# Bias products as weighted sums on GpSimd, weight maxima in slices, and the output weights' product in other banks

## The reference

```python
h = jnp.maximum(_layernorm(x, axis=-1), 0.0)
q = h @ Wq.T + bq
k = key @ Wk.T + bk
v = value @ Wv.T + bv
scores = jnp.einsum('nd,md->nm', q, k) / scale          # scale = 4096 ** 0.5
adj_scores = scores * adj_matrix
adj_scores = jnp.where(jnp.abs(adj_scores) < 1e-05, -1000000000.0, adj_scores)
prob = jax.nn.softmax(adj_scores, axis=-1)
out = x + jnp.einsum('nm,md->nd', prob, v) @ Wm.T + bm
```

## Time and profile before

| | us |
|---|---|
| median of 3 runs | 1592.18 |
| the profiled execution | 1591.07 |
| its span in the profile | 1589.3 |
| PE busy | 1567.6 (99%) |
| DVE busy | 993.6 (63%) |
| ACT busy | 609.3 (38%) |
| POOL busy | 101.8 (6%) |

### The profile page before, as it was taken

The page is one execution under the profiler, slowest core; times in us unless marked ns, Lnnn a source line. Parts: engine busy times, 40 slices in busy tenths (PEclk is TensorE's granted clock), DMA queues, the critical chain, the costliest instruction groups (busy, mean ns, idle before and its releaser), DMA issues.

```text
span 1589.3 us, 23599 instructions
## 1 busy us (share of the span) xinstructions
PE 1567.6 (99%) x7246; PEld 720.3 (45%) x7246; DVE 993.6 (63%) x2325; ACT 609.3 (38%) x964; POOL 101.8 (6%) x178
## 2 busy tenths in 40 slices
PE   8899999999999999999999999999999999999998
PEld 5543444444444444444444444444444444444443
DVE  4779766656666656656665656666566666666652
ACT  4667333333333333333333333333333333333332
POOL 0132000000000000000000000000000000000000
PEclk9999999999999999999999999999999999999999
DMA  9724555655555455555545555545555554555545
GB/s 348 254 53 107 121 130 117 130 126 125 119 125 124 116 136 119 124 125 127 117 116 137 119 123 122 130 120 119 135 123 119 121 129 119 126 129 124 116 95 106
DMA packets 430287, 205.46 MB, mean 129 GB/s; under 512 B 375088, under 2 KB 375344, under 8 KB 430128
## 3 DMA queue, kind: packets, MB, share of 16 engines
q1 hardware_dynamic: 429680, 204.80, 54.2%
q10 hardware_dynamic: 576, 0.27, 0.1%
HBM read 105.13 MB, written 8.39 MB: 71 GB/s over the span
## 4 chain that ended last, share of the span: by engine, by line
PE 93%; DVE 2%; DMA 2%; issue 1%; ACT 1%; SPq 1%; POOL 0%; DVEq 0%; ACTq 0%; POOLq 0%
PE R L559 13%; PE R L560 13%; PE R L561 13%; PE S L559 13%; PE S L560 13%; PE S L561 13%; PE M L559 3%; PE M L561 3%; PE M L560 3%; DMA pT<-ph 1%; PE R L638 1%; PE R L671 0%; DMA xq<-in_x_dram 0%; DVE small L1142 0%; PE W L709 0%
## 5 line engine op out<-in xcount | busy, mean ns | idle before, releaser
L941 ACT ACTIVATE drop<-Zbuf 128x512 f32<-128x512 f32 x256 | 161.2, 630 | 808.4 <-DVE cmx L1234 808.3
L1225 DVE SCALAR_TENSOR_TENSOR Zbuf<-S,rs,adjb 128x512 f32<-128x512 f32 x256 | 192.0, 750 | 346.4 <-PE S L561 342.6
L559 PE MATMUL R<-Vbuf,pT 128*128 128x512 f16 x1008 | 383.0, 380 | 6.9 <-issue 5.5
L560 PE MATMUL S<-Kbuf,qT 128*128 128x512 f16 x1024 | 388.9, 380 | 0.0
L559 PE MATMUL S<-Kbuf,qT 128*128 128x512 f16 x1024 | 388.8, 380 | 0.0
L561 PE MATMUL S<-Kbuf,qT 128*128 128x512 f16 x1024 | 388.7, 380 | 0.0
L560 PE MATMUL R<-Vbuf,pT 128*128 128x512 f16 x1008 | 382.9, 380 | 0.0
L561 PE MATMUL R<-Vbuf,pT 128*128 128x512 f16 x1008 | 382.8, 380 | 0.0
L1234 DVE CUSTOM_DVE_ANT_0 Zbuf<-drop,Zbuf 128x512 f32<-128x512 f32 x256 | 175.8, 687 | 0.0
L1285 DVE TENSOR_SCALAR drop<-drop,rs 128x512 f32<-128x512 f32 x256 | 142.1, 555 | 33.4 <-ACT drop L941 33.1
L947 ACT ACTIVATE Zbuf<-Zbuf,smx 128x1024 f32<-128x1024 f32 x128 | 157.4, 1230 | 4.5 <-DVE smx L1248 1.6
(11 more groups left out here) (189 smaller groups left out, 1194.2 us busy)
## 6 DMA issues: line engine op xcount, KB each, us to landing
adjb<-in_adj_dram SPq DMA_DIRECT2D x256, 256.0 KB, 2.8
xq<-in_x_dram SPq DMA_DIRECT2D x32, 256.0 KB, 2.8
Kbuf<-in_L_gnn_key_dram SPq DMA_DIRECT2D x8, 1024.0 KB, 14.3
xr<-in_x_dram SPq DMA_DIRECT2D x32, 256.0 KB, 2.8
...
```

Of the source, the lines that this page charges most:

```text
L559: nc.tensor.matmul(ps, lhs[0], rhs[0], start=start, stop=False)
L560: nc.tensor.matmul(ps, lhs[0], rhs[1], start=False, stop=False)
L941: nc.scalar.activation(drop[:, :], Zbuf[:, s.p, s.c * CW:(s.c + 1) * CW], ACT.Abs).then_inc(abs_ready, 1)
L1225: nc.vector.scalar_tensor_tensor(out=z, in0=S[s.j % 2][:, :], scalar=rs[:, r, 3, s.c // 2:s.c // 2 + 1], in1=adjb[:, s.j % ADJ_SLOTS, :], ...
```

## The change

The bias columns are no longer widened. The three bias vectors are loaded as rows on one partition, TensorE turns them into columns with 12 one-row matmuls between 8 and 4 warm-up matmuls (20 before), and VectorE copies the columns out. GpSimd multiplies the four row groups of a weight matrix by its four bias columns and adds them up (`weighted_sum`: four multiplications and three additions of 128 x 512), and one fp32 matmul against ones (`sum_over_partitions`) gives the finished row; this holds for `qbias`, `wrow` and bv Wm^T. The product bq.bk is one product by ones as well. bm is loaded later, by SyncE.

VectorE takes the weight maxima in eight reductions of 512 columns as the weights arrive, instead of two of 2048 after the last, and it does so ahead of the first block's layer norm. The maxima of A go through bank W[1], and those of VB through O[0]. The key scales K2 and K3 are flattened, reduced and spread in other steps: the spread stands one step later than the flattening. Wm is transposed in step 6, bv Wm^T finished in step 10, B formed in steps 7 to 10 in the banks M1, W[0], O[1] and M0, and split in steps 10 and 11; the VB maximum is in steps 8 and 9. The first two adjacency tiles are loaded ahead of key chunk 5, the second query block ahead of Wm, and values in smaller portions a step later in the queue.

```diff
-        wrow, once = W[1], M0[:, 0:1]
...
+        wrow, once = W[1], W[1][:, 0:1]
...
-            FILLS += ["Wm^T"] * ND * (g == 6) + [g] * ND
-        FILLS += ["bias"] + ["B"] * ND
+            FILLS += [g] * ND
+        FILLS += ["Wm^T"] * ND + ["B"] * ND
...
+        B_BANKS = [M1, W[0], O[1], M0]
         def bank_of(n):
-            if FILLS[n] == "bias":
-                return M1
-            return ROUND.get(n // ND, RING)[(n - (FILLS[n] == "B")) % ND]
+            if FILLS[n] == "B":
+                return B_BANKS[n - FILLS.index("B")]
+            return ROUND.get(n // ND, RING)[n % ND]
...
-        WM_STEP, BIAS_STEP, B_STEPS, B_OUT = 4, 5, {6: 0, 7: 1, 8: 2, 9: 3}, 10
-        VB_LARGEST, VB_SCALES = 7, 8
-        V_LOADS = [(1, 2), (3, 4), (5, 6), (7, 8, 9)]
+        WM_STEP, SUM_STEP, BIAS_STEP, B_STEPS, B_OUT = 6, 7, 10, {7: 0, 8: 1, 9: 2, 10: 3}, (10, 11)
+        VB_LARGEST, VB_SCALES = 8, 9
+        V_LOADS = [(1,), (2,), (3,), (4, 5), (6, 7, 8, 9)]
...
+        def top_bank(what):
+            return {"A": W[1], "VB": O[0]}.get(what, M1)
...
             for g in range(NC):
+                if g == ADJ_TURN:
+                    for t in range(ADJ_SLOTS):
+                        load_adj(0, t, t)
                 sp.dma_start(k_stage(g), kv[g, :, :, :]).then_inc(k_in[g], 16)
-            for t in range(ADJ_SLOTS):
-                load_adj(0, t, t)
+            sp.wait_ge(dot_done, 1)
+            sp.dma_start(xq[:, :], x[P:2 * P, :]).then_inc(x_in, 16)
...
+            def weighted_sum(total, term, weights, k, bias, done):
+                nonlocal steps
+                if k == 0:
+                    nc.gpsimd.tensor_scalar(total, weights, bias[:, 0:1], None, ALU.mult).then_inc(sum_steps, 1)
+                    steps += 1
+                else:
+                    wait(pool, sum_steps, steps)
+                    nc.gpsimd.tensor_scalar(term, weights, bias[:, k:k + 1], None, ALU.mult).then_inc(sum_steps, 1)
+                    steps += 1
+                    pool.wait_ge(sum_steps, steps)
+                    last = nc.gpsimd.tensor_tensor(total, total, term, ALU.add)
+                    if k == ND - 1:
+                        last.then_inc(done, 1)
+                    else:
+                        last.then_inc(sum_steps, 1)
+                        steps += 1
...
+            pool.wait_ge(bcol, 1)
+            for k in range(ND):
+                pool.wait_ge(w_in[k], 32)
+                weighted_sum(sum_q, term, Wk_sb[:, k, :], k, bqc, q_sum)
+                if k == ND - 2:
+                    rstd_of(1)
...
+            pool.wait_ge(q_sum, 1)
+            for k in range(ND):
+                if k == 1:
+                    root_of("K0")
+                weighted_sum(sum_w, term, Wq_sb[:, k, :], k, bkc, w_sum)
             root_of("K1")
...
+                if isinstance(s.t, int) and s.t == SUM_STEP:
+                    pool.wait_ge(wm_seen, 1)
+                    pool.wait_ge(start_act, ND)
+                    pool.wait_ge(w_sum, 1)
+                    for k in range(ND):
+                        weighted_sum(sum_o, term_o, WmT[:, k, :], k, bvc, o_sum)
...
                     filled(last)
+            def sum_over_partitions(ps, part):
...
             def out_bias():
-                ps = bank_of(fill)
+                pe.wait_ge(o_sum, 1)
+                pe.wait_ge(v_small, 1)
                 pe.wait_ge(q_small, Q_SMALL + 1)
-                pe.wait_ge(start_act, ND)
-                for k in range(ND):
-                    last = nc.tensor.matmul(ps[:, :], bvrep[:, k, :], WmT[:, k, :], start=(k == 0), stop=(k == ND - 1))
-                filled(last)
+                sum_over_partitions(O[0][:, :], sum_o).then_inc(bias_mm, 1)
...
             pe.wait_ge(ident_ready, 2)
-            for n in range(20):
+            for n in range(8):
+                nc.tensor.matmul(S[1][:, 0:P], ident[:, :], ident[:, :], start=True, stop=True)
+            pe.wait_ge(b_in, 48)
+            for n, b in enumerate(bias_rows):
+                for k in range(ND):
+                    last = nc.tensor.matmul(M0[:, n * ND + k:n * ND + k + 1], b.rearrange("a (p k) -> a k p", k=ND)[:, k, :], one,
+                                            start=True, stop=True)
+            last.then_inc(bcol_mm, 1)
+            for n in range(4):
                 nc.tensor.matmul(S[1][:, 0:P], ident[:, :], ident[:, :], start=True, stop=True)
             for k in range(ND - 1):
                 pe.wait_ge(w_in[k], 32)
                 round_a(k, range(ND))
             pe.wait_ge(w_in[ND - 1], 32)
+            flat_max("A", wmax[:, 0:2], 2)
             round_a(ND - 1, range(0, 1))
-            pe.wait_ge(ident_ready, 2)
...
+            flat_max("K0", kst[:, 6, 0:1], 1)
+            spread_max("A")
+            pe.wait_ge(bcol, 1)
             transpose_x(1)
-            round_a(ND - 1, range(1, 3))
-            spread_max("A")
-            round_a(ND - 1, range(3, 4))
-            flat_max("K0", kst[:, 6, 0:1], 1)
+            round_a(ND - 1, range(1, ND))
+            pe.wait_ge(q_sum, 1)
+            sum_over_partitions(S[1][:, :], sum_q).then_inc(aside_mm, 1)
+            pe.wait_ge(a_small, 1)
+            pe.wait_ge(bdot_ready, 2)
+            sum_over_partitions(once, bdot[:, ND:ND + 1]).then_inc(aside_mm, 1)
+            spread_max("K0")
             transpose_key(0)
-            spread_max("K0")
-            pe.wait_ge(reps_ready, 1)
-            for k in range(ND):
...
+                    if s.t == 3:
+                        spread_max("K3")
...
-                    if s.t == 0:
-                        spread_max("K2")
                     if s.t == 2:
-                        spread_max("K3")
+                        flat_max("K3", kst[:, 6, 3:4], 1)
...
-            dve.wait_ge(b_in, 48)
-            dve.wait_ge(ident_ready, 2)
-            for k in range(ND):
-                nc.vector.tensor_scalar(bqrep[:, k, :], ident[:, :], 0.0, bqc[:, k:k + 1], ALU.mult, ALU.add)
-                nc.vector.tensor_scalar(bkrep[:, k, :], ident[:, :], 0.0, bkc[:, k:k + 1], ALU.mult, ALU.add)
-                last = nc.vector.tensor_scalar(bvrep[:, k, :], ident[:, :], 0.0, bvc[:, k:k + 1], ALU.mult, ALU.add)
-            last.then_inc(reps_ready, 1)
...
+            nc.vector.tensor_reduce(bdot[:, ND:ND + 1], bdot[:, 0:ND], X, ALU.add).then_inc(bdot_ready, 1)
             for k in range(ND):
                 dve.wait_ge(w_in[k], 32)
-            largest(0, (Wq_sb, Wk_sb)).then_inc(part_max, 1)
-            widest_product("A", 2)
-            scale_of(ast, a_small, "A", 400, 2.0 ** -40, 2 * TOP / D, D / (2 * TOP) / HS)
+                for n, w in enumerate((Wq_sb, Wk_sb)):
+                    nc.vector.tensor_reduce(wpart[:, n * ND + k:n * ND + k + 1], w[:, k, :], X, ALU.max,
+                                            apply_absolute_value=True).then_inc(w_part, 1)
+            dve.wait_ge(w_part, 2 * ND)
+            nc.vector.tensor_reduce(wmax[:, 0:2], wpart.rearrange("p (n k) -> p n k", n=2), X, ALU.max).then_inc(part_max, 1)
...
+            dve.wait_ge(xn_ready, 1)
+            nc.vector.tensor_scalar(xq[:, :], xq[:, :], rstd[:, 2:3], None, ALU.mult).then_inc(xs_ready, 1)
             dve.wait_ge(k_sum, 2)
             largest_keys("K0", 0, 1)
+            widest_product("A", 2)
+            widest("K0", 1).then_inc(wide_done, 1)
+            scale_of(ast, a_small, "A", 400, 2.0 ** -40, 2 * TOP / D, D / (2 * TOP) / HS)
+            h_low(1)
...
+                if isinstance(s.t, int) and s.t == BIAS_STEP:
+                    add_bias()
...
-                if isinstance(s.t, int) and s.t == B_OUT:
-                    for k in range(0, ND, 2):
-                        low_of_pair(*[B_sb[:, h, k:k + 2, :].rearrange("p k d -> p (k d)") for h in range(2)], b_scale)
+                if isinstance(s.t, int) and s.t == B_OUT[0]:
+                    for k in range(2):
+                        low_of(B_sb[:, 0, k, :], B_sb[:, 1, k, :], b_scale)
+                if isinstance(s.t, int) and s.t == B_OUT[1]:
+                    low_of_pair(*[B_sb[:, h, 2:4, :].rearrange("p k d -> p (k d)") for h in range(2)], b_scale)
```

207 lines of the change are left out of this document (105 added, 102 removed).

## The result

The changed kernel takes 1587.33 us in the median of seven runs (1586.20 to 1590.18), beside 1592.41 (1590.88 to 1593.90) for the kernel before: ratio 0.997, 95% interval 0.9961 to 0.998. That is 5 us less, where 12.5 were forecast, and above the range of 1575 to 1586.5. It is faster, as forecast, by less than half as much.

What follows compares the result with a forecast made beforehand. PE's queue was taken as the bound: its start, work and gaps. Less work, idle and half rate, with new gaps added, gave 11.6 us of lead, plus 2.2 of half rate, 13.8; less 1.4, 12.4: 1579.7 us, range 1575 to 1586.5.

Steps and rivals of the forecast that it cites:

- the price of the one-row matmuls: Start, ahead of A: 24 records at 0.119 us, 2.8 us in all, so that A starts at 8.85.
- rival 4: Start: small matmuls and a late bias row leave PE's clock low into A's rounds, 5 us lost, 1585; chance 0.11.
- signs of being wrong: GpSimd sum over 14 us, PE wait over 2 us in steps 12 to 19, or A's first round after 10 us.
- The rest of the start: From A to step 0: first projection at 27.7 us instead of 33.77, step 0's scores at 36.7 instead of 44.02.
- Steps 0 to 11: Scores' starts from 42.0 us (step 1) to 106.8 (step 11); lead 7 in step 1, some 16 in step 8.
- Rival 2: Gaps up to the first value product close better than added: lead 16 us, time 1576; chance 0.12.
- rival 3: GpSimd's sums ahead of step 0 and VB's root become the bound, kernel slower: lead -4 us, 1596; chance 0.04.
- PE work: Bias products and narrow product on PE: 8.2 and 0.75 us removed, in all 8.9 us less.
- The weight maxima: Ahead of A's maximum: DVE's maxima in slices end near 14 us, and the 1.1 us gap at 20.14 goes.
- The bank change: First value product no longer waits for B's split: the 5.5 us gap goes, and 2.2 us of half rate.
- lay off 1.4: From step 10 on DVE doesn't quite carry PE's lead of 13.8 us; 1.4 off, 12.4 kept.
- rival 1: Steps 10 to 19: DVE and ScalarE, not PE, set the pace; lead 7 to 9.5 us, 1583 to 1585; chance 0.18.

Runs made afterwards that it cites:

- e7: The changed kernel with its 12 one-row matmuls reading 128 neighbouring elements of their row instead of every fourth; 1583.39 us in one run.
- e2: The changed kernel with 20 warm-ups ahead of the 12 one-row matmuls and none behind them; 1588.45 us, ratio 0.9974.
- e1: The changed kernel with the bias columns by three small column loads and 20 warm-ups, without the 12 one-row matmuls; 1580.56 us, ratio 0.9923.
- e6: e1's kernel with half of key 1's transposes moved ahead of the transposes of the first queries' row; 1579.26 us, ratio 0.9914.
- e11: e6's kernel with e9's edit and K3's maximum taken ahead of the key's splits in step 2; 1575.55 us, ratio 0.9896.
- e9: e6's kernel with the second queries' row split ahead of step 13's value tiles, not behind them; 1577.22 us, ratio 0.99.
- e12: e6's kernel without the last six of the seven GpSimd instructions of the third weighted sum; 1579.27 us, ratio 0.9915.
- e14: e1's kernel with each product by ones issued four times, restoring the PE work of before; 1589.12 us, ratio 0.9984.
- e8: e1's kernel with the maxima of Wq and Wk taken whole when all slices have landed; 1581.00 us, ratio 0.9924.
- e5: The changed kernel with the first value product waiting until the first two of B's banks are split; 1587.04 us, ratio 0.9965.
- e13: e11's kernel with e5's added wait ahead of the first value product; 1575.65 us, ratio 0.99.

## Why the prediction was wrong, point by point

**The step that failed: the price of the one-row matmuls.** "then 12 one-column matmuls, 24 records at the 0.119 of the narrow product (0.95 / 8) 2.8, then 4 warm-ups, 0.9: A starts at 1.71 + 7.1 = 8.85". They took 5.69 us, and A started at 12.81 (the sum as written gives 8.81). The narrow product has its 128 x 128 weights without gaps; these matmuls read one partition with a stride of 16 bytes. e7 shows that the stride is the 2.9 us, e2 that the clock isn't. To this comes what they did to the clock, 2.2 us in all: the 4 warm-ups took 1.87 for 0.9, and six records of A's first round 3.97 for 2.74. My bound for this place was 2.7 us, for a late load, and I had the clock in rival 4 at a chance of 0.11. That rival ("the start gains nothing", 1585) is what happened, with its place and half of its mechanism right: the bias rows were in time (PE has no idle time ahead of 5.25), the small matmuls were the cause. I had written it as a mishap and not asked for its price from a row of the same shape, which the trace of before does not have.

Two of the prediction's own signs of being wrong were there: A's first round after 10 us (12.81), and a wait of PE of over 2 us in steps 12 to 19 (2.05 at step 16). Nor was PE without idle time after 160, as it had said: 1.50 us at 167.94 and 0.86 at 308.83.

**The rest of the start was right.** With the columns loaded, e1 has A's maximum at 18.24, the first projection at 26.72 and step 0's scores at 37.26, where the forecast, once its A at 8.85 is put at 7.85, gives 18.2, 26.7 and 35.7. The 1.6 us too few between projection and step 0 are half rate behind the wait of 1.44 for the queries' scaling (key 1's transposes take 2.60 there for 1.53), which e6 removes.

**Steps 0 to 11** came out near the estimates. The masking of step 10 was forecast at 105.5, or 104.5 with A at 7.85, and is at 105.20 in e1; in the changed kernel it is 110.50, late by the start. The gap for K3 was forecast at 2.0 and is 2.3. PE waits for no key, weight or value tile that has not landed, so the other DMAs cost PE nothing, as taken; in e1 DVE waits 0.65 for the adjacency tile of step 2. Rival 2 (1576, the gaps close better) did not come by itself; e11 reaches its time (1575.55) with column loads and three edits more.

**GpSimd** kept up, as forecast, rival 3 is refuted. A multiplication takes 1.56 and an addition 1.27, not 1.70 and 1.40; the third sum runs from 89.11 to 99.81, 10.7 us for my 11.6 (in e1 from 83.79, forecast 83.2). PE waits 0.8 for VB's root, not 2.7. On DVE the prediction's reading of the earlier trace rows was too kind to one sort of GpSimd instruction. Beside the third sum's multiplications DVE's maximum takes 0.75 and 0.68, which is next to nothing more, and beside the scaling of the values 0.95. But beside GpSimd instructions with two inputs, which are the sums' additions and GpSimd's splits of value tiles, a DVE instruction with two inputs, or a copy, waits until the other is over. Here are GpSimd's split and DVE's split of the second queries' row in the changed kernel, then the latter in e9:

```profile
136.90 1.40 POOL L593 TENSOR_TENSOR Vbuf<-Vbuf 128x512 f16<-128x512 f32 x1 [3.23 <-ACT Vbuf L968]
```

```profile
137.38 1.47 DVE L1409 TENSOR_TENSOR row<-xq,row 128x512 f16<-128x512 f32 x1
```

```profile
128.10 0.68 DVE L1335 TENSOR_TENSOR row<-xq,row 128x512 f16<-128x512 f32 x1
```

The other side of the comparison is e12, which leaves the additions out: a copy of 128 x 4 numbers takes 0.16 us there and 1.25 in e6 beside the second addition, and the product of two single numbers ahead of VB's root 0.15 and 0.65 beside the third. In the changed kernel the maximum takes 0.98 beside each of three splits by GpSimd, and in the kernel before it did so too. The rule of the Trainium skill (SBUF — State Buffer, "Who interferes with whom") that a DVE instruction with two SBUF inputs and a GpSimd instruction that reads SBUF exclude each other for the whole instruction is borne out by these rows, but not by those beside a multiplication, where the maximum is over before it. In the stretch of the third sum it cost DVE 1.6 us; e12 puts the price of six of the 21 instructions at the end at 0. The 0.8 us by which the second queries' row is held up (1.47 for 0.68) lies on the path of the wait at step 16; the kernel before had it too (1.35).

**PE work** of 8.9 us less counted in full, as taken: e14's 8.6.

**The weight maxima** by slices were credited with the 1.1 us gap of the earlier trace rows. e8 puts the slices at 0.4. The gap had come from the layer norm ahead of the maxima, where DVE waited 2.51 us for x; the change moves the maxima ahead of it.

**The bank change** was credited with the 5.5 us gap and 2.2 of half rate, 7.7 us of the sum. e5 and e13 put the part that a wait can put back, 3 us of lead, at 0. The lead at the second value product is there (10.4 us), but then PE waits for the queries' row and the last value tiles. Here the term "lay off 1.4" was too small: from the second value product to the span the lead falls by 6.1 (10.4 to 4.3, of which 1.0 at 308.83) and in e1 by 4.8 (15.6 to 10.8). This is rival 1, "DVE and ScalarE, not PE, set the pace from step 10 to 19"; it had 0.18. It is right for what PE alone gains there and wrong for what all engines gain before.

**The errors in sum.** e1 shows the forecast without its failed step. With A at 7.85 and not 8.85 the forecast is 1578.7 for it, and it took 1580.56. That it is so near is luck in part: the gaps up to the first value product were 0.9 us smaller than I added them (109.65 for 110.5), the loss behind it was 3.4 larger, and the median lies 2.1 above the profile's span, where 2.9 had been added.

What is open: the exact share of the change's late steps (B's rounds and Wm's transposes one or two steps later) was not tried by itself, nor were the `ho` row's waits of 1.5 us at 167.94 and 0.86 at 308.83, the place of the weight maxima, and the rest of the old gap ahead of the first value product, which no run put back whole (5.5 us and half rate; in e5 PE waits 3.0 and keeps its rate).
